# Softplus sums and a quantiser step shared between ScalarE, GpSimd and VectorE in a four-stage block kernel

## The chip, the cores and the metric
One core of a Trainium2 chip. The metric is the device time of one execution in microseconds (us): the median of the runs. The engines are TensorE (PE), VectorE (DVE), ScalarE (ACT), GpSimd (POOL) and SyncE (SP), which issues most DMAs.

## What is computed
The reference is a block of four layers on x (4 x 256 tokens of 256), each added with a gate tanh(g):

```python
x = x + tanh(g_xattn[0]) * L0_xattn(layernorm(x), ctx)   # softmax attention, keys and queries from ctx
x = x + tanh(g_ffn[0])   * L0_ffn(layernorm(x))          # silu(gate) * up, rms norm, projection
x = x + tanh(g_xattn[1]) * L1_xattn(ctx, layernorm(x))   # state space layer, 256 channels x 16 states
x = x + tanh(g_ffn[1])   * L1_ffn(layernorm(x))          # 64 experts, top 8
# two parts of it that the change touches:
delta = softplus(einsum('er,brl->bel', dt_proj_w, dt_lo) + dt_proj_b)      # of L1_xattn
scale = clip(mean(abs(w_g)), 1e-8); w_hat = clip(round(w_g / scale), -1, 1) * scale   # of L0_ffn, groups of 64
```

Softplus is computed as relu(v) + ln(1 + e) with e = exp(-|v|), plus a correction for what rounding 1 + e loses: c = (1 + e) - 1 - e, and delta = ln(1 + e) + (relu(v) - c). The ternary weights are computed in bf16: scale - |w|, a comparison of that with |w|, the sum of the two (the scale as rounded), then sign times mask, then times the scale.

## The kernel before
It is written by hand in one program per engine. Every wait and every order is explicit, and each engine runs its list in order, so an instruction that waits holds all behind it. A semaphore wait (`wait_ge`) names the count that must have been reached.

The time falls into a preparation (to about 70 us), the scan of the state space layer with the gated feed-forward layer beside it (to 200 us), the routing (to 230 us), and the 64 experts (to the end). The change lies in the preparation. Data is held with 128 rows on the partitions; the channels of the state space layer are two halves h of 128, with 1024 tokens each in the free dimension.

VectorE's list there: for half 0 the convolution (`convolve`, L1449 and three L1452, in place on `u`), the group sums and scales of the first weight part (`scales(0)`, L1458, L1460), eight maxima of the attention energies (L1489, out of PSUM), `convolve(1)`, `scales(1)`, the reciprocal of the softmax sums (L1493), then the quantiser: `rest_and_mask` (L1466 the difference scale - |w|, L1468 the comparison) for both parts, `restored` (L1474) for both, `quantised(0)` (L1481, L1483); then x1 (L1516, eight), statistics (L1417, L1420), the softplus steps `softplus_rest` (L1504 1 + e, L1506 the correction, L1509 relu minus it) for half 0, the same again for the second half of the tokens and half 1, then delta (L1526) for both halves, `quantised(1)`, four rests of the normalised tokens (L1534) and the first delta times u (L1539). From there `state(k)` runs 64 times: the product of delta u and B (L1556, in PSUM) and the scan (L1561), which needs ScalarE's decay (L853).

ScalarE's list: absolute weights (L743, L750), exponentials of the attention (L758), silu of u (L763, its second half after `convolve(1)`), normalising copies (L768, after L1493), signs of the weights (`signs`, L774), transposed attention (L779), Abs and Relu of the dt projection (L791, L792), Exp of both halves (L795), `signs(1)`, `normalised_rows(0)` (L785, waits for `nmr`, L1426), Ln (L800), `normalised_rows(1)`, `keep_high` (L818), two weight copies (L811), then `decay(0)` and on; `keep_middle` (L824) and a silu (L891) lie between the decays. An activation table is loaded (ACT_TABLE_LOAD) wherever the loaded set lacks the next function.

GpSimd's list: constants, `ln_rstd(1)` and `ln_rstd(2)` (L568, and L570, a power of -0.5) in two halves of the tokens each, two memsets, `rest_low` (L589), then the products of states and C (L602, `product`), with squares, hidden units and delta times u between.

TensorE's list: the attention energies (L1038), the x projection (L1045, which needs silu of u of both halves), attention transposes (L1052, which need L768), the dt projection (L1058), attention times values (L1065), weight transposes (L1077, L1089), token transposes (L1025), then the feed-forward layer (`gate_up`, L1153), which needs `rest_low`.

The second GpSimd operand of the difference is the scale, read with a stride of zero over pairs:

```python
in_pairs = "p (g n two) -> p g n two"
q_pairs, v_pairs = (v.rearrange(in_pairs, n=GROUP // 2, two=2) for v in (q_abs, q_v))
def over_group(part2):
    g = q_groups[part2]
    return part(q_scale[:, g.start, 0:1], (2, g.stop - g.start), (0, GROUP // 2), (1, 2))
```

## Time and profile before

| what | value |
|---|---|
| median of 3 runs | 410.79 us (410.63 to 410.82) |
| profiled execution | 411.59 us |
| its span, first to last instruction | 409.8 us |
| granted TensorE clock, mean | 0.928 |

The profiled execution is one of its own, and its parts are read against its own 411.59 us. A timeline row is a run of equal instructions: start, time from the first start to the last end, engine, line, operation, output and inputs, shapes, count, and in brackets how long the engine was idle before and who ended that. An instruction that is stopped after it has been issued shows that in its own duration. An instruction's end overlaps the next one's start a little, so sums are made from start to start.

### The profile page before, as it was taken

To read this page: it belongs to the slowest core of one execution; us is meant where nothing else is said; L and a number is where in the kernel's file an instruction comes from. 1 tells how busy PE (TensorE), PEld (TensorE's weight loads), DVE (VectorE), ACT (ScalarE), POOL (GpSimd) and SP (SyncE) were. 2 spreads that over 40 slices of the span, in tenths; PEclk is the share of its full clock that TensorE was granted. 3 is DMA by queue.
4 is the path that set the end of the run, shared out by engine and by line. 5 is a ranking of instruction groups with operands and counts; after the bars stand their busy time and mean duration, and the time that the engine had idled before them with its cause. 6 is when DMAs were issued, how large, how long until landed. Compare 5 with 4: busy or idle time off the path is not lost.

```text
span 409.8 us, 7559 instructions
## 1 busy us (share of the span) xinstructions
PE 335.7 (82%) x2206; PEld 269.0 (66%) x2217; DVE 305.5 (75%) x694; ACT 258.2 (63%) x528; POOL 260.6 (64%) x213
## 2 busy tenths in 40 slices
PE   4948944697798799799893299999999998999980
PEld 2433733365566567567793287998999897998960
DVE  2999999899999999999998937445453544454365
ACT  0998989999888888987265354445444443544410
POOL 4200041789978878887514678778878778787830
PEclk9997875799999989999899589999999999999995
DMA  8930520666435777331396349899888998865466
GB/s 233 375 123 14 155 102 0 219 229 220 155 114 186 258 264 251 129 136 51 85 268 175 112 103 247 204 230 225 214 217 213 233 224 194 215 146 91 84 123 226
DMA packets 59132, 72.17 MB, mean 176 GB/s; under 512 B 6802, under 2 KB 43458, under 8 KB 59106
## 3 DMA queue, kind: packets, MB, share of 16 engines
q1 hardware_dynamic: 49104, 56.04, 43.8%
q0 software_dynamic: 8832, 15.74, 19.2%
q8 instruction: 12, 0.20, 0.2%
q10 hardware_dynamic: 1170, 0.08, 0.2%
q14 instruction: 14, 0.11, 0.1%
HBM read 61.75 MB, written 10.09 MB: 175 GB/s over the span
## 4 chain that ended last, share of the span: by engine, by line
PE 43%; ACT 20%; DVE 15%; DMA 10%; issue 7%; POOL 2%; SPq 0%; DVEq 0%; POOLq 0%; ACTq 0%
PE bank L1319 12%; PE bank L1357 9%; PE bank L1312 5%; ACT ssm L853 4%; PE bank L1299 3%; DVE bank L1556 3%; ACT L853 3%; DMA ssm<-routed,idx 3%; ACT L891 3%; DVE ssm L1561 2%; DMA ssm<-bc_rows 2%; PE bank L1153 2%; DMA du<-sums 2%; DMA B_last<-bc_rows 2%; PE bank L1065 2%
## 5 line engine op out<-in xcount | busy, mean ns | idle before, releaser
L602 POOL TENSOR_TENSOR ssm<-ssm,arena 128x1024 f32<-128x1024 f32 x31 | 73.1, 2358 | 18.5 <-issue 10.2
L1561 DVE TENSOR_TENSOR_SCAN ssm<-ssm,bank 128x512 f32<-128x512 f32 x64 | 78.1, 1221 | 4.0 <-issue 1.8
L675 POOL DMA_INDIRECT ssm<-routed,idx x64 | 65.2, 1019 | 21.8 <-issue 14.6
L1784 DVE SCALAR_TENSOR_TENSOR ssm<-ssm,bank 128x96 f32<-128x96 f32 x64 | 20.0, 313 | 75.9 <-ACT ssm L965 75.7
L686 POOL DMA_INDIRECT sums<-ssm,idx x40 | 65.6, 1639 | 13.9 <-issue 10.4
L1319 PE MATMUL bank<-ssm,wguT 128*128 128x256 bf16 x576 | 72.4, 272 | 0.3 <-DVE ssm L1776 0.3
L1319 PEld LDWEIGHTS bank<-ssm,wguT 128*128 128x128 bf16 x576 | 56.0, 97 | 12.3 <-DVE ssm L1776 0.6
L965 ACT ACTIVATE ssm<-bank 128x96 f32<-128x96 f32 x64 | 16.0, 250 | 74.1 <-PE bank L1357 74.1
L1357 PE MATMUL bank<-arena,ssm 128*128 (+1 forms) x256 | 53.3, 331 | 1.6 <-ACT ssm L948 1.1
L1153 PE MATMUL bank<-xs,wguT 128*128 128x512 bf16 x182 | 44.4, 393 | 11.1 <-POOL xs L589 4.6
L853 ACT ACTIVATE ssm<-delta,A_sb 128x510 f32<-128x510 f32 x64 | 43.9, 713 | 6.8 <-DVE ssm L1561 6.7
L1095 PE MATMUL bank<-ident,ssm 128*128 128x128 f32 x256 | 35.1, 284 | 11.1 <-ACT bc_buf L860 5.8
L1357 PEld LDWEIGHTS bank<-arena,ssm 128*128 128x128 f32 x256 | 40.8, 193 | 3.4 <-issue 2.2
L568 POOL TENSOR_SCALAR rstd<-mv 128x4 f32<-128x4 f32 x8 | 2.7, 332 | 59.6 <-DVE mv L1420 48.4
L1153 PEld LDWEIGHTS bank<-xs,wguT 128*128 128x128 bf16 x192 | 18.8, 101 | 32.7 <-issue 8.9
L1095 PEld LDWEIGHTS bank<-ident,ssm 128*128 128x128 f32 x256 | 30.2, 146 | 15.1 <-ACT bc_buf L860 6.5
L1312 PE MATMUL bank<-arena,ssm 96*128 (+1 forms) x128 | 38.6, 383 | 0.5 <-ACT ssm L952 0.5
L1299 PE MATMUL bank<-ident,ssm 128*128 128x128 f32 x128 | 25.9, 285 | 5.9 <-DMA ssm<-routed,idx 5.9
L948 ACT ACTIVATE ssm<-bank 128x256 f32<-128x256 f32 x64 | 24.5, 383 | 9.2 <-PE bank L1299 9.1
L1556 DVE TENSOR_TENSOR bank<-bank,ssm 128x512 f32<-128x512 f32 x44 | 29.9, 679 | 0.1
L958 ACT ACTIVATE ssm<-bank 128x256 f32<-128x256 f32 x64 | 24.5, 383 | 6.4 <-PE bank L1312 3.5
L1299 PEld LDWEIGHTS bank<-ident,ssm 128*128 128x128 f32 x128 | 22.9, 198 | 6.8 <-DMA ssm<-routed,idx 6.6
(225 smaller groups left out, 663.7 us busy)
## 6 DMA issues: line engine op xcount, KB each, us to landing
ssm<-bc_rows SPq DMA_DIRECT2D x22, 512.0 KB, 3.7
arena<-bc_rows SPq DMA_DIRECT2D x16, 512.0 KB, 4.9
arena<-in_L_ffn_gate_proj SPq DMA_DIRECT2D x32, 192.0 KB
arena<-in_L_ffn_up_proj SPq DMA_DIRECT2D x32, 192.0 KB
arena<-in_L_ffn_down_proj SPq DMA_DIRECT2D x32, 192.0 KB
B_last<-bc_rows SPq DMA_DIRECT2D x10, 512.0 KB, 3.6
sums<-zero_f SPq DMA_DIRECT2D x1, 2304.0 KB, 14.1
arena<-in_L_ffn_w_gate_up SPq DMA_DIRECT2D x1, 2048.0 KB, 11.4
```

The lines of the kernel that those rows point to most:

```text
L602: pool.tensor_tensor(prod[:, a:b, :], hs[:, a:b, :], C_all[:, 2 * (q % 8):2 * (q % 8) + 2, :], ALU.mult).then_inc(s.prod_ok, 1)
L675: pool.indirect_dma_start(out=xe[:, k, :], out_offset=None, in_=routed, in_offset=bass.IndirectOffsetOnAxis(ap=idx2[:, k, 0:1], axis=0)).t ...
L686: pool.indirect_dma_start(out=sums, out_offset=bass.IndirectOffsetOnAxis(ap=idx2[:, k, 1:2], axis=0), in_=ye[:, k, :], in_offset=None, com ...
L853: act.activation(part(dA[:, k % 3, 0:1], (L, 2), (1, L - 1), offset=1), part(delta[:, h, 0:1], (L, 2), (1, L - 1), offset=th * 512 + 1), A ...
L1095: ins = pe.matmul(bank[3][:, t * P:t * P + P], prod[:, a, t * P:t * P + P], ident[:, :], start=first and t == 0, stop=False, is_transpose= ...
L1153: ins = pe.matmul(bank[(7, 0)[g]][:, :], wguT[:, kc, hc * P + g * H:hc * P + g * H + P], xs[:, part3, kc, th * 512:th * 512 + 512], start= ...
L1299: ins = pe.transpose(of_input()[:, t * P:t * P + P], part(xe[:, k, 0:1], (2, P), offset=t), ident[:, :])
L1312: pe.matmul(of_result(), hhT[0:I, k % 2, :], w_dn[:, bass.ds(slot, 1), :], start=True, stop=True).then_inc(s.m_y_ps, 1)
L1319: ins = pe.matmul(bank[4 + j // 2][:, (j % 2) * D:(j % 2) * D + D], places[:, which, j, :], ye_parts[:, which, c, :], start=False, stop=Fa ...
L1357: ins = pe.matmul(bank[1][:, 0:2 * I], xeT[:, k % 2, t * P:t * P + P], w_gu[:, :, bass.ds(slot, 1), t * I:(t + 1) * I], start=t == 0, stop ...
L1556: dve.tensor_tensor(x[:, :], bank[5][:, :], B_buf[q % 3][:, k % 2, :], ALU.mult).then_inc(s.dBu_ok, 1)
L1561: dve.tensor_tensor_scan(hs[:, k % 4, :], dA[:, k % 3, :], x[:, :], 0.0, ALU.mult, ALU.add).then_inc(s.scan_ok, 1)
```

## The change
- ScalarE loads the set of the exponential table ahead of its first wait, and the set `natural_log_exp_and_others` ahead of the Exp of softplus.
- 1 + e of both halves is made by ScalarE (Identity with a bias of 1) behind both Exp; VectorE's L1504 goes. VectorE keeps both corrections; half 0's subtraction and sum stay on VectorE, half 1's go to GpSimd, behind `ln_rstd(2)`. `decay` waits for half 0 at first and for half 1 at step 16.
- The quantiser's difference of the first weight part (4096 bf16 on 128 partitions) is made by GpSimd, behind `ln_rstd(1)`. The second part's stays on VectorE, behind the first comparison.
- The maxima and x1 are taken a PSUM bank at a time: four instructions of 512 for eight of 256.
- Semaphore counts follow (`q_step` without the differences, `q_rest`, `sp_one` and `delta_second` new; TensorE and ScalarE wait for the same data under the new counts).

Cut from the diff: the new semaphores' lines and the renumbered waits of ScalarE (`keep_high`) and TensorE.

```diff
--- before.py
+++ after.py
...
@@ -571,14 +574,26 @@
 
             ln_rstd(1)
 
+            g0 = q_groups[0]
+            pool.wait_ge(s.q_scales, 2)
+            pool.wait_ge(s.q_cast, 1)
+            pool.tensor_tensor(v_pairs[:, g0], over_group(0), q_pairs[:, g0], ALU.subtract).then_inc(s.q_rest, 1)
+
             ln_rstd(2)
+
+            pool.wait_ge(s.sp_c, 2)
+            pool.wait_ge(s.sp_relu, 4)
+            pool.tensor_tensor(Bbc[:, 1, :], du[:, 1, :], Bbc[:, 1, :], ALU.subtract).then_inc(s.delta_second, 1)
+            pool.wait_ge(s.delta_second, 1)
+            pool.wait_ge(s.sp_ln, 2)
+            pool.tensor_tensor(delta[:, 1, :], Cbc[:, 1, :], Bbc[:, 1, :], ALU.add).then_inc(s.delta_second, 1)
             pool.wait_ge(s.xm_ps, NT)
             for th in halves:
                 pool.memset(acc_sq[:, th, :], 0.0).then_inc(s.acc_ok, 1)
 
             def rest_of_du(h, t):
 
-                pool.wait_ge(s.delta_sb, 2)
+                pool.wait_ge(*((s.delta_sb, 1), (s.delta_second, 2))[h])
                 pool.wait_ge(s.u_sb, 2)
                 pool.tensor_tensor(du[:, h, t], delta[:, h, t], u[:, h, t], ALU.mult).then_inc(s.du_sb, 1)
 
...
@@ -715,6 +730,7 @@
             NCOLS = 16 * 4
 
 
+            act.preload_act_table_set("exp_and_others")
             act.wait_ge(s.c_pad, 1)
             for k in range(4):
                 act.wait_ge(s.xin_ps, k + 1)
...
@@ -754,7 +770,7 @@
                 act.activation(xnT[:, k % 2, (k // 2) * 512:(k // 2) * 512 + 512], bank[(5, 6, 7, 0)[k]][:, :], ACT.Copy).then_inc(s.xn1T_sb, 1)
 
             for j in range(NT):
-                act.wait_ge(s.en_max, 2 * (j // 2) + 2)
+                act.wait_ge(s.en_max, j // 2 + 1)
                 act.activation(att[:, j, :], bank[1 + j // 2][:, (j % 2) * L:(j % 2) * L + L], ACT.Exp, bias=nmax[:, j:j + 1],
                                accum_out=asum[:, j:j + 1]).then_inc(s.att_exp, 1)
 
...
@@ -790,9 +806,13 @@
                 src = bank[(7, 0, 5, 6)[k]][:, :]
                 act.activation(delta[:, h, c * 512:c * 512 + 512], src, ACT.Abs, bias=cols[:, 2 + h:3 + h]).then_inc(s.sp_abs, 1)
                 act.activation(du[:, h, c * 512:c * 512 + 512], src, ACT.Relu, bias=cols[:, 2 + h:3 + h]).then_inc(s.sp_relu, 1)
+            act.preload_act_table_set("natural_log_exp_and_others")
             for h in halves:
                 act.wait_ge(s.sp_abs, 2 * h + 2)
                 act.activation(delta[:, h, :], delta[:, h, :], ACT.Exp, scale=-1.0).then_inc(s.sp_exp, 1)
+            for h in halves:
+                act.wait_ge(s.sp_exp, h + 1)
+                act.activation(Bbc[:, h, :], delta[:, h, :], ACT.Identity, bias=1.0).then_inc(s.sp_one, 1)
             signs(1)
             normalised_rows(0)
             for h in halves:
...
@@ -842,12 +862,14 @@
             keep_quantised(1)
 
             act.wait_ge(s.Aneg, 2)
-            act.wait_ge(s.delta_sb, 2)
+            act.wait_ge(s.delta_sb, 1)
             act.wait_ge(s.reset_ok, 1)
 
             def decay(k):
 
                 th, h, n, t = of_step(k)
+                if k == DS:
+                    act.wait_ge(s.delta_second, 2)
                 if k >= 3:
                     act.wait_ge(s.scan_ok, k - 2)
                 act.activation(part(dA[:, k % 3, 0:1], (L, 2), (1, L - 1), offset=1),
...
@@ -1409,11 +1431,11 @@
 
                 for c in chunks:
                     if update:
-                        for j in range(4 * c, 4 * c + 4):
-                            update(j)
+                        for b in range(2 * c, 2 * c + 2):
+                            update(b)
                     for j in range(4 * c, 4 * c + 4):
-                        if update:
-                            dve.wait_ge(updated, j + 1)
+                        if updated:
+                            dve.wait_ge(updated, j // 2 + 1)
                         dve.bn_stats(stats[:, j, :], x_res[:, j, :]).then_inc(s.ln_stats, 1)
                     for j in range(4 * c, 4 * c + 4):
                         dve.wait_ge(s.ln_stats, 16 * (n - 1) + 4 * c + j + 1)
...
@@ -1462,31 +1484,32 @@
             def rest_and_mask(part2):
 
                 t, g = q_cols[part2], q_groups[part2]
-                dve.wait_ge(s.q_scales, 2 * part2 + 2)
-                dve.tensor_tensor(v_pairs[:, g], over_group(part2), q_pairs[:, g], ALU.subtract).then_inc(s.q_step, 1)
-                dve.wait_ge(s.q_step, 2 * part2 + 1)
+                if part2 == 1:
+                    dve.wait_ge(s.q_scales, 4)
+                    dve.tensor_tensor(v_pairs[:, g], over_group(1), q_pairs[:, g], ALU.subtract).then_inc(s.q_rest, 1)
+                dve.wait_ge(s.q_rest, part2 + 1)
                 dve.tensor_tensor(q_m[:, t], q_v[:, t], q_abs[:, t], ALU.is_lt).then_inc(s.q_step, 1)
 
             def restored(part2):
 
                 t = q_cols[part2]
-                dve.wait_ge(s.q_step, 2 * part2 + 2)
+                dve.wait_ge(s.q_step, part2 + 1)
                 dve.tensor_tensor(q_v[:, t], q_v[:, t], q_abs[:, t], ALU.add).then_inc(s.q_step, 1)
 
             def quantised(part2):
 
                 t = q_cols[part2]
                 dve.wait_ge(s.q_cast, part2 + 3)
-                dve.wait_ge(s.q_step, 6)
+                dve.wait_ge(s.q_step, 4)
                 dve.tensor_tensor(q_sign[:, t], q_sign[:, t], q_m[:, t], ALU.mult).then_inc(s.q_step, 1)
-                dve.wait_ge(s.q_step, 2 * part2 + 7)
+                dve.wait_ge(s.q_step, 2 * part2 + 5)
                 dve.tensor_tensor(q_r[:, t], q_v[:, t], q_sign[:, t], ALU.mult).then_inc(s.q_step, 1)
 
             convolve(0)
             scales(0)
-            for j in range(NT):
-                dve.wait_ge(s.en_ps, 2 * (j // 2) + 2)
-                dve.tensor_reduce(nmax[:, j:j + 1], bank[1 + j // 2][:, (j % 2) * L:(j % 2) * L + L], AX.X, ALU.max, negate=True).then_inc(s.en_max, 1)
+            for b in range(B):
+                dve.wait_ge(s.en_ps, 2 * b + 2)
+                dve.tensor_reduce(nmax[:, 2 * b:2 * b + 2], bank[1 + b][:, :].rearrange("p (a m) -> p a m", m=L), AX.X, ALU.max, negate=True).then_inc(s.en_max, 1)
             convolve(1)
             scales(1)
             dve.wait_ge(s.att_exp, NT)
...
@@ -1498,34 +1521,34 @@
 
             quantised(0)
 
-            def softplus_rest(h, meanwhile):
-
-                dve.wait_ge(s.sp_exp, h + 1)
-                dve.tensor_scalar(Bbc[:, h, :], delta[:, h, :], 1.0, None, ALU.add).then_inc(s.sp_c, 1)
-                dve.wait_ge(s.sp_c, 3 * h + 1)
+            def correction(h):
+
+                dve.wait_ge(s.sp_one, h + 1)
                 dve.scalar_tensor_tensor(out=Bbc[:, h, :], in0=Bbc[:, h, :], scalar=-1.0, in1=delta[:, h, :], op0=ALU.add, op1=ALU.subtract).then_inc(s.sp_c, 1)
-                dve.wait_ge(s.sp_c, 3 * h + 2)
-                dve.wait_ge(s.sp_relu, 2 * h + 2)
-                dve.tensor_tensor(Bbc[:, h, :], du[:, h, :], Bbc[:, h, :], ALU.subtract).then_inc(s.sp_c, 1)
-                meanwhile()
 
             dve.wait_ge(s.tg_sb, 1)
 
-            def x1(j):
-                dve.wait_ge(s.xm_ps, 2 * (j // 2) + 2)
-                dve.scalar_tensor_tensor(out=x_res[:, j, :], in0=bank[1 + j // 2][:, (j % 2) * L:(j % 2) * L + L], scalar=tg[:, 0:1],
-                                         in1=x_res[:, j, :], op0=ALU.mult, op1=ALU.add).then_inc(s.x1_sb, 1)
+            def x1(b):
+                dve.wait_ge(s.xm_ps, 2 * b + 2)
+                dve.scalar_tensor_tensor(out=x_res[:, 2 * b:2 * b + 2, :], in0=bank[1 + b][:, :].rearrange("p (a m) -> p a m", m=L), scalar=tg[:, 0:1],
+                                         in1=x_res[:, 2 * b:2 * b + 2, :], op0=ALU.mult, op1=ALU.add).then_inc(s.x1_sb, 1)
 
             statistics(2, x1, s.x1_sb, (0,))
-            softplus_rest(0, lambda: mean_over_deviation(2, 0))
-            statistics(2, x1, s.x1_sb, (1,))
-            softplus_rest(1, lambda: mean_over_deviation(2, 1))
-            for h in halves:
-                dve.wait_ge(s.sp_c, 3 * h + 3)
-                dve.wait_ge(s.sp_ln, h + 1)
-                dve.tensor_tensor(delta[:, h, :], Cbc[:, h, :], Bbc[:, h, :], ALU.add).then_inc(s.delta_sb, 1)
+            correction(0)
+            x1(2)
+            mean_over_deviation(2, 0)
+            x1(3)
+            statistics(2, None, s.x1_sb, (1,))
+            correction(1)
+            dve.wait_ge(s.sp_c, 1)
+            dve.wait_ge(s.sp_relu, 2)
+            dve.tensor_tensor(Bbc[:, 0, :], du[:, 0, :], Bbc[:, 0, :], ALU.subtract).then_inc(s.sp_c, 1)
+            mean_over_deviation(2, 1)
             quantised(1)
-            dve.wait_ge(s.q_step, 10)
+            dve.wait_ge(s.sp_c, 3)
+            dve.wait_ge(s.sp_ln, 1)
+            dve.tensor_tensor(delta[:, 0, :], Cbc[:, 0, :], Bbc[:, 0, :], ALU.add).then_inc(s.delta_sb, 1)
+            dve.wait_ge(s.q_step, 8)
             dve.memset(part(dA[:, 0, 0:1], (512, 3), (L, 2), (1, 1)), 0.0).then_inc(s.reset_ok, 1)
 
             for k in range(4):
...
```

## Rows read from the trace of the kernel before

**Rows 1.** The page: part 1 (busy us, share of the span), part 5 (costliest groups).
```profile
PE 335.7 (82%) x2206; PEld 269.0 (66%) x2217; DVE 305.5 (75%) x694; ACT 258.2 (63%) x528; POOL 260.6 (64%) x213
...
L602 POOL TENSOR_TENSOR ssm<-ssm,arena 128x1024 f32<-128x1024 f32 x31 | 73.1, 2358 | 18.5 <-issue 10.2
```

**Rows 2.** Timeline, VectorE, 24 to 35 us: start us, us, instruction.
```profile
24.68 2.73 DVE L1489 TENSOR_REDUCE nmax<-bank 128x1 f32<-128x256 f32 x8
27.33 0.80 DVE L1449 TENSOR_SCALAR u<-xin,conv_sb,cols 128x1024 f32<-128x1024 f32 x1
34.43 0.19 DVE L1493 RECIPROCAL rasum<-asum 128x8 f32<-128x8 f32 x1
34.54 2.24 DVE L1466 TENSOR_TENSOR ssm<-q_scale,arena 128x4096 bf16<-128x4096 bf16 x1
```

**Rows 3.** Timeline, VectorE, 54 to 82 us.
```profile
54.60 1.22 DVE L1509 TENSOR_TENSOR bc_buf<-du,bc_buf 128x1024 f32<-128x1024 f32 x1
70.11 0.70 DVE L1556 TENSOR_TENSOR bank<-bank,ssm 128x512 f32<-128x512 f32 x1
81.85 1.22 DVE L1561 TENSOR_TENSOR_SCAN ssm<-ssm,bank 128x512 f32<-128x512 f32 x1 [1.81 <-issue]
```

**Rows 4.** Timeline, ScalarE, 13 to 59 us; in brackets the idle time before.
```profile
13.29 0.60 ACT L721 ACTIVATE xin<-bank 128x512 f32<-128x512 f32 x1 [0.38 <-PE bank L1004]
32.12 1.06 ACT L763 ACTIVATE u<-u 128x1024 f32<-128x1024 f32 x1 [0.46 <-DVE u L1452]
34.66 1.71 ACT L768 ACTIVATE wguT<-wguT,rasum 128x256 f32<-128x256 f32 x4 [1.48 <-DVE rasum L1493]
50.25 2.00 ACT L795 ACTIVATE delta<-delta 128x1024 f32<-128x1024 f32 x2
55.93 2.08 ACT L785 ACTIVATE xw<-x_res,nmr,rstd 128x256 f32<-128x256 f32 x4 [1.88 <-DVE nmr L1426]
58.02 1.28 ACT L800 ACT_TABLE_LOAD   x1
```

**Rows 5.** The chain of waits, 68 to 80 us: start us, us, what.
```profile
68.20 1.28 ACT L853
79.75 1.28 ACT L853
```

**Rows 6.** Timeline, GpSimd: the price of its steps.
```profile
52.81 0.57 POOL L568 TENSOR_SCALAR rstd<-mv 128x4 f32<-128x4 f32 x1 [38.92 <-DVE mv L1420]
74.06 2.37 POOL L602 TENSOR_TENSOR ssm<-ssm,arena 128x1024 f32<-128x1024 f32 x1 [0.37 <-DVE ssm L1561]
86.76 1.15 POOL L589 TENSOR_TENSOR xs<-xnT,xs 128x512 bf16<-128x512 f32 x1
219.65 0.67 POOL L651 TENSOR_TENSOR xw<-delta,mask_b 128x256 f32<-128x256 f32 x1 [2.92 <-ACT delta L931]
```

**Rows 7.** Timeline, GpSimd and VectorE where they overlap, 53 to 231 us.
```profile
53.47 1.99 POOL L570 TENSOR_TENSOR rstd<-rstd,mhalf 128x4 f32<-128x4 f32 x1
...
196.83 2.35 POOL L602 TENSOR_TENSOR ssm<-ssm,arena 128x1024 f32<-128x1024 f32 x1
198.67 1.59 DVE L1617 TENSOR_TENSOR ssm<-ssm,arena 128x1024 f32<-128x1024 f32 x1
...
221.71 0.61 POOL L658 TENSOR_TENSOR xw<-xw,rasum 128x256 f32<-128x256 f32 x1
221.76 0.57 DVE L1426 SCALAR_TENSOR_TENSOR nmr<-mv,rstd 128x4 f32<-128x4 f32 x1 [0.39 <-POOL rstd L570]
...
226.32 1.71 DVE L1705 TENSOR_SCALAR bc_buf<-du 128x384 f16<-128x384 int16 x2
226.83 1.08 POOL L668 IOTA xin<- 128x1024 f16 x1
230.46 2.22 DVE L1705 TENSOR_SCALAR bc_buf<-du 128x384 f16<-128x384 int16 x11
```

**Rows 8.** Busy us by engine, 32 to 36 us; granted clock third from last.
```profile
32.00:36.00 4.00, 4.00 (x5) 0.78 (x5) 3.96 (x5) 2.40 (x5) 0.00 (x0) 0.50 0.00 0
```

More of the change, by code:

```diff
@@ L113, in __init__ @@
         self.q_scales = sem("q_scales")
+        self.q_rest = sem("q_rest")
         self.attT_ps = sem("attT_ps")
@@ L116, in __init__ @@
         self.sp_c = sem("sp_c")
+        self.sp_one = sem("sp_one")
+        self.delta_second = sem("delta_second")
         self.sp_ln = sem("sp_ln")
@@ L816, in keep_high @@
                 act.wait_ge(s.xn2T_ps, k + 1)
-                act.wait_ge(s.q_step, 8)
+                act.wait_ge(s.q_step, 6)
                 act.activation(xs[:, 0, kc, c], bank[1 + k][:, :], ACT.Copy).then_inc(s.xs_hi, 1)
@@ L1070, in _ @@
             pe.wait_ge(s.c_ident, 2)
-            pe.wait_ge(s.q_step, 8)
+            pe.wait_ge(s.q_step, 6)
             qv = q_r[:, q_cols[0]].rearrange("p (c d) -> p c d", d=D)
@@ L1078, in _ @@
                 ins.then_inc(s.quantT_ps, 1)
-            pe.wait_ge(s.x1_sb, NT)
+            pe.wait_ge(s.x1_sb, NT // 2)
             transpose_tokens(2, (1, 2, 3, 4), s.xn2T_ps)
-            pe.wait_ge(s.q_step, 10)
+            pe.wait_ge(s.q_step, 8)
             pv = q_r[:, q_cols[1]].rearrange("p (c h) -> p c h", h=H)
```

## The prediction
> **What bounds the kernel now.** The page's first part says little here: VectorE is busy 75% of the span [rows 1], and that is an average over stages. The change works between 24 and 80 us, so the views to read are the timelines of the engines over that stretch and the chain of waits. VectorE has no gap from 24.5 us to its scan at 81.85 us, the sixth [rows 2, 3]. ScalarE has only short waits, each for VectorE: 0.46 us for the second half's convolution, 1.48 us for the reciprocal of the softmax sums (L1493), 1.88 us for `nmr` [rows 4]. The chain agrees: ScalarE and TensorE carry it to about 49 us, then VectorE (x1, statistics, softplus), then ScalarE with a table load at 68.20 and one at 79.75 [rows 5]. The two engines run almost level, so a saving on VectorE alone buys little before 49 us and most of itself after. GpSimd is idle for 38.92 us, to 52.81 us [rows 6]. After 81.85 us nothing of the change is left and VectorE is dense again: what the sixth scan gains or loses is what the whole time gains or loses.
>
> **The change part by part.** All times are of the profiled execution, 411.59 us, of which 409.8 is its span; it lies 0.8 above the median of 410.79.
>
> **The first table preload**: the load before ScalarE's first copy moves ahead of a wait. The third copy waits 0.38 us for TensorE as it is [rows 4], so TensorE sets this start: 0. Without that cover at most 1.28 us would be gained.
>
> **The maxima**: eight reduces of 256 take 2.65 us from start to start (24.68 to 27.33 [rows 2]), 0.33 each. VectorE's two-input steps take 0.70 us for 512 elements and 1.22 for 1024 [rows 3], 1.02 ns for each more, so 256 more elements add 0.27: four take 4 x 0.60 = 2.40, -0.25. **x1 in pairs**: four fixed parts of about 0.13 fewer, -0.5, half of it before the first statistics. **Semaphore renumbering**, TensorE's waits on x1 and the `decay(16)` wait for the second half (29 us after the first state step): 0, the data is long there.
>
> **The quantiser's first difference on GpSimd** takes L1466's 2.24 us from VectorE [rows 2]. What does it cost GpSimd? A two-input f32 step takes 0.67 us for 256 elements (rows of 64) and 2.37 for 1024 [rows 6], 2.2 ns for each more; 4096 make 9.1 us. No row has an all-bf16 one: with one bf16 input and a bf16 output 512 take 1.15 [rows 6], 7% below that line (8.5 for ours); sixteen times the short one is 10.7. I take 8.9, nearer to the f32 line, and keep 8.5 to 10.7. It starts when the first scales are written, just after the first maximum starts at 24.68, so runs 24.85 to 33.75. The result is first needed at 34.2: on the face of it, it is hidden.
>
> **Whether it may run beside VectorE** is the step that decides. The collisions of [rows 7] show what happens when VectorE meets a GpSimd instruction that streams. L1617 (two SBUF inputs, 1024) started 198.67, GpSimd's product (196.83 + 2.35) ended 199.18, and it took 1.59 us where the same shape takes 1.22 (L1509 [rows 3]); it ended 1.08 after GpSimd. L1426, four elements, took 0.57, ending 0.01 after the GpSimd multiply of 221.71. A single-input f16 step (L1705) takes 0.2 in a row of 11 (2.22 us); the two beside a multiply's end and a 1.08 us iota took 1.71. Each time VectorE stood until GpSimd's instruction was over. What did not collide: VectorE's steps with one operand in PSUM. The 31 products average 2358 ns [rows 1] beside scans and state products, which all have one, and the one at 74.06 took 2.37 [rows 6]. In reverse GpSimd's `pow` of four elements, started at 53.47, ended at 55.46, 0.9 us after VectorE's L1506 had made way for L1509 at 54.60 [rows 3, 7].
> So I sort what stands behind 24.85 us on VectorE. The four maxima read PSUM: free, to 24.68 + 2.40 = 27.1. Then comes `convolve(1)`: L1449 does 1024 f32 elements in 0.80 us [rows 2], less than any two-input step (1.22), so like L1705 it runs in a faster single-input mode, and the three L1452 have two SBUF inputs. They stand until 33.75: 6.65 us, minus the 0.14 us of start-up that L1617 overlapped.
> The Trainium skill (SBUF — State Buffer, "SBUF: two separate sides") says the two engines' shared port pair is an exclusive lock held for the full instruction. The longest such hold in the trace is about 1 us; whether one of 9 us is held throughout no row shows, and the page's rule says yes. Without such a hold the sum would be that of rival A.
>
> **From there, by start-to-start times of before.** L1449 to the second scales took 27.33 to 34.43 [rows 2], 7.1 us; from 33.75, less 0.14, L1493 starts 40.7: +6.3. ScalarE's second silu and the normalising copies follow it: copies at 40.95 instead of 34.66. TensorE's second half of x_proj starts near 39.4 at the lower of the clock's levels, 1.2 GHz (0.50 in 32 to 36 us [rows 8], after TensorE had idled); three of its four matmuls then remain, and five half ones fill those 4 us, 0.85 each, so done 44.5; ScalarE wants it at 44.6. `signs(0)` starts 45.2, +6.4. From there ScalarE has no waits to the last Relu: 55.3.
> VectorE: masks, difference of part 1, restores to 49.0, `quantised(0)` to 53.5 (signs ready 48.8), two x1 to 54.9, statistics 56.4.
> ScalarE: load 56.6, two Exp 58.5, and now 1+exp: two more of 1024. Two Exp take 2.00 us [rows 4], so +0.95 each: 59.5 and 60.4; `signs(1)` 62.2. VectorE's `correction(0)` must wait for 59.5, a new stall of 3 us, which the late ScalarE makes and not the arithmetic; 60.8. Then x1(2), `nmr` 61.6, x1(3), statistics 63.85, `correction(1)` 65.1, the first half's subtraction 66.3. VectorE is rid of the two L1504 and of the second half's two sums, 2.4 us.
> ScalarE: rows of half 0 to 64.3, Ln to 66.25 without the load at 58.02, -1.28 [rows 4], diagonals 66.85.
> GpSimd: statistics ready 63.85; its `pow` is held by VectorE's two steps and ends 0.9 after the last of them, 67.2, as at 53.47. Next in its queue is the second half's subtraction, 2.36 us, whose inputs are ready; VectorE's `nmr` needs a semaphore first. That is the situation of L1426 at 221.76. So `nmr` 69.6 instead of 67.3. The last addition (2.36) then falls between the two steps of `quantised(1)`.
> ScalarE: rows of half 1 69.75 to 71.75, high parts 73.75, two weight copies 75.65, `decay(0)` 75.7 without the load at 68.20 (69.50 before: +6.2). VectorE: 69.65, L1481 70.9, GpSimd's addition 73.2, L1483 74.4, delta 75.6, four L1534 78.0, L1539 78.7, first state product 78.75 (70.11 before: +8.6). VectorE reaches the sixth scan 9.26 + 0.7 after that, 88.75; ScalarE reaches decay(5), behind decay(3), which waits for the first scan, at 87.7. Against 81.85 with 1.81 us of waiting: **+6.9 us**. C loads behind `signs(1)` (62.2 instead of 54) land 7 us before the first product; the other waits in GpSimd's queue (`rest_low` at 77.5) are behind nothing longer.
>
> The two saved loads are certain only if one set holds Exp and Ln. The loads at 58.02 and 68.20 show that they were taken from two sets. The Trainium skill (ScalarE: Activation LUTs, "Table sets: the hidden batching unit") says the named set has both; no row shows it. Without that the sum is +6.9 + 1.28 + 1.28 at most.
>
> Sum: 411.59 + 6.9 = 418.5 profiled, and by the same 0.8 a median of **417.7**.
>
> **The rivals.** **A, GpSimd and VectorE do not meet** (a long instruction lets go between pieces): the difference ends 33.75 before its use at 34.2. VectorE then gains 0.25 + 2.24 + 0.25 ahead of the first statistics, but `correction(0)` waits for ScalarE's 53.2, `signs(1)` ends 56.0 and the first rows start as before (55.93 [rows 4]). The gain is made after: Ln without load, rows of half 1 at 60.9 instead of 62.26, `decay(0)` 67.05 instead of 69.50, state 67.9 instead of 70.11. -2.4: 408.4. Against it: three collisions of [rows 7]; for it: none is longer than 1.1 us. Chance 9%.
> **B, only the long one holds.** `nmr` and `quantised(1)` slip past the two 1024 steps (`nmr` 67.3, state near 74.3): 6.9 - 2.7 = +4.2, 415.0. It would need VectorE to win each handover, where [rows 7] show it lose at 221.76. 14%.
> **C, the difference is far slower on GpSimd** than 10.7 us, its rows being pairs of bf16 beside a stride of zero. From 8.9 us on, each us is a us of stall. At twice the price, 17.8 us, 417.7 + 8.9 = 426.6. 10%.
> **D, the change does not do what it says** (preload ignored, one load back, ScalarE pieces longer): +1.3 to +2.6, 419 to 420.3. 5%.
>
> **How the numbers follow.** The forecast has 62%. Its bounds: the difference at 8.5 to 10.7 us (-0.4, +1.8), TensorE late at the low clock (x1 up to 0.7 later), B's mixture (-2.7) and D's loads (+2.6): 413.5 to 421. The range 413.0 to 421.5 leaves out A and C, about 2 in 10. 0.2% is 0.8 us, about what a measurement here can tell. Faster is A with something for other ways to gain, 0.10; same 0.03, a mixture between A and B; slower 0.87.
>
> **What would show it.** L1449 of the second half lasting some 7 us, or VectorE idle as long before it, ending with GpSimd's difference; that one's own length (8.5 to 10.7). L1493 at 40.7. `correction(0)` waiting for ScalarE. L1426 of the second half stretched by 2.3 us behind a GpSimd step. No table load between Exp and `decay(0)`. First state product near 78.8, sixth scan near 88.7. If L1449 keeps 0.80 us at 27.1, the prediction is wrong at its root, and A holds.

## The result and the profile after

The changed kernel takes 416.8 us (415.14 to 418.47, four runs) against 410.81 us (four runs of the kernel before beside them): a ratio of 1.0142 with an interval of 1.0101 to 1.0183, so +6.0 us, between +4.1 and +7.5. The forecast was 417.7 with a range of 413.0 to 421.5, and "slower" at 0.87. The profiled execution took 415.14 us (span 413.3); it is the quickest of the four, and this matters below.

The page, part 1 and the products of part 5, beside [rows 1]; and the busy table of 32 to 36 us beside [rows 8], in the same columns.

```profile
PE 338.0 (82%) x2206; PEld 266.7 (65%) x2217; DVE 307.4 (74%) x681; ACT 257.5 (62%) x528; POOL 272.8 (66%) x216
...
L617 POOL TENSOR_TENSOR ssm<-ssm,arena 128x1024 f32<-128x1024 f32 x31 | 73.1, 2359 | 19.4 <-DVE ssm L1584 11.4
...
32.00:36.00 4.00, 1.58 (x2) 0.00 (x0) 3.89 (x5) 0.00 (x0) 0.00 (x0) 0.50 0.00 0
```

VectorE ran 13 instructions fewer and was busy 1.9 us *longer*; GpSimd ran three more and was busy 12.2 us longer. The products beside the scans kept their length (2359 against 2358 ns), so the scan stage was left alone, as its operands in PSUM suggested. In 32 to 36 us ScalarE did nothing at all: it waited for the second half's convolution.

The place of the loss is VectorE's timeline, here beside [rows 2] (the maxima are now L1512, L1449 is L1471, L1493 is L1516), with GpSimd's difference.

```profile
24.25 2.47 DVE L1512 TENSOR_REDUCE nmax<-bank 128x2 f32<-128x512 f32 x4
26.64 5.37 DVE L1471 TENSOR_SCALAR u<-xin,conv_sb,cols 128x1024 f32<-128x1024 f32 x1
32.04 3.92 DVE L1474 SCALAR_TENSOR_TENSOR u<-xin,conv_sb,u 128x1024 f32<-128x1024 f32 x3
...
38.31 0.20 DVE L1516 RECIPROCAL rasum<-asum 128x8 f32<-128x8 f32 x1
...
24.41 7.05 POOL L580 TENSOR_TENSOR ssm<-q_scale,arena 128x4096 bf16<-128x4096 bf16 x1 [10.77 <-DVE q_scale L1482]
```

L1471, a step of 0.80 us before, lasts 5.37 and ends at 32.01, 0.55 us after GpSimd's difference (24.41 + 7.05 = 31.46). The timeline shows no idle time: a held instruction looks like a long one. The four maxima out of PSUM, under the same GpSimd instruction, were not held (2.47 us, the forecast's 2.40).

ScalarE, beside [rows 4]; GpSimd from 62 us, beside [rows 6, 7]; then VectorE from 57 us to the sixth scan, beside [rows 3].

```profile
5.86 1.28 ACT L733 ACT_TABLE_LOAD   x1 [5.86 <-issue]
...
12.76 0.60 ACT L737 ACTIVATE xin<-bank 128x512 f32<-128x512 f32 x1 [0.26 <-PE bank L1026]
...
36.00 1.06 ACT L779 ACTIVATE u<-u 128x1024 f32<-128x1024 f32 x1 [4.48 <-DVE u L1474]
...
53.13 1.28 ACT L809 ACT_TABLE_LOAD   x1
...
56.33 1.99 ACT L815 ACTIVATE bc_buf<-delta 128x1024 f32<-128x1024 f32 x2
...
61.99 1.99 ACT L820 ACTIVATE bc_buf<-delta 128x1024 f32<-128x1024 f32 x2
...
72.92 1.34 ACT L875 ACTIVATE ssm<-delta,A_sb 128x510 f32<-128x510 f32 x2
```

```profile
62.89 1.86 POOL L573 TENSOR_TENSOR rstd<-rstd,mhalf 128x4 f32<-128x4 f32 x1
64.73 2.33 POOL L586 TENSOR_TENSOR bc_buf<-du,bc_buf 128x1024 f32<-128x1024 f32 x1
67.15 3.29 POOL L589 TENSOR_TENSOR delta<-bc_buf 128x1024 f32<-128x1024 f32 x1
...
74.86 2.71 POOL L604 TENSOR_TENSOR xs<-xnT,xs 128x512 bf16<-128x512 f32 x2 [3.50 <-ACT xs L844]
```

```profile
57.41 1.23 DVE L1527 SCALAR_TENSOR_TENSOR bc_buf<-bc_buf,delta 128x1024 f32<-128x1024 f32 x1 [3.25 <-ACT bc_buf L815]
...
64.79 2.29 DVE L1448 SCALAR_TENSOR_TENSOR nmr<-mv,rstd 128x4 f32<-128x4 f32 x1 [0.94 <-POOL rstd L573]
67.01 1.21 DVE L1504 TENSOR_TENSOR xs<-xs,ssm 128x2048 bf16<-128x2048 bf16 x1
68.26 3.26 DVE L1506 TENSOR_TENSOR arena<-ssm,xs 128x2048 bf16<-128x2048 bf16 x1
...
74.98 1.58 DVE L1562 TENSOR_TENSOR bank<-delta,u 128x512 f32<-128x512 f32 x1
76.66 0.70 DVE L1579 TENSOR_TENSOR bank<-bank,ssm 128x512 f32<-128x512 f32 x1
...
86.62 1.22 DVE L1584 TENSOR_TENSOR_SCAN ssm<-ssm,bank 128x512 f32<-128x512 f32 x1
```

Three more steps of VectorE are stretched beside a GpSimd instruction: `nmr` of four elements 2.29 us, L1506 3.26 instead of 1.22, delta times u (L1562) 1.58 instead of 0.69. The load in front of the first decay (68.20 in [rows 5]) is gone from ScalarE's timeline; the one of 79.75, behind the silu between the decays, is still there, at 84.21. The chain of waits can be followed back only to 73.86 us in this trace; its second row is the stretched delta times u:

```profile
73.86 1.20 DVE xnT L1557 x2
75.06 1.51 DVE bank L1562
```

The first state product starts 6.55 us later than before (76.66 against 70.11) and the sixth scan 4.77 later (86.62 against 81.85 [rows 3]); before, 1.81 us of the way between them had been waiting.

### The profile page after: what moved, and what is told of

Its sections match the earlier page's. It is cut to its first block, busy times and chain, and to the rows that moved or that the text cites. A ratio compares the mean times of both kernels' runs of the same rounds, so it can differ in the third digit from the quotient of the medians.

```text
span 413.3 us, 7551 instructions
## 1 busy us (share of the span) xinstructions
PE 338.0 (82%) x2206; PEld 266.7 (65%) x2217; DVE 307.4 (74%) x681; ACT 257.5 (62%) x528; POOL 272.8 (66%) x216
## 4 chain that ended last, share of the span: by engine, by line
PE 36%; DVE 12%; ACT 12%; issue 8%; DMA 7%; POOL 5%; SPq 0%; DVEq 0%; POOLq 0%; ACTq 0%
PE bank L1341 10%; PE bank L1379 8%; PE bank L1334 5%; ACT ssm L875 3%; PE bank L1175 3%; DVE bank L1579 3%; PE bank L1321 3%; DVE ssm L1584 3%; DMA ssm<-routed,idx 3%; ACT L875 2%; ACT L913 2%; POOL ssm L690 2%; PE bank L1117 2%; PE bank L1327 1%; DMA du<-sums 1%
## 5 line engine op out<-in xcount | busy, mean ns | idle before, releaser
L617 POOL TENSOR_TENSOR ssm<-ssm,arena 128x1024 f32<-128x1024 f32 x31 | 73.1, 2359 | 19.4 <-DVE ssm L1584 11.4
L701 POOL DMA_INDIRECT sums<-ssm,idx x40 | 65.9, 1648 | 13.9 <-issue 10.7
L1175 PE MATMUL bank<-xs,wguT 128*128 128x512 bf16 x182 | 47.3, 412 | 7.1 <-POOL xs L604 2.8
L1117 PE MATMUL bank<-ident,ssm 128*128 128x128 f32 x256 | 33.8, 278 | 11.0 <-ACT bc_buf L882 5.7
L1117 PEld LDWEIGHTS bank<-ident,ssm 128*128 128x128 f32 x256 | 29.4, 143 | 15.4 <-POOL ssm L617 6.9
L1321 PE MATMUL bank<-ident,ssm 128*128 128x128 f32 x128 | 25.9, 284 | 5.6 <-DMA ssm<-routed,idx 5.5
L1321 PEld LDWEIGHTS bank<-ident,ssm 128*128 128x128 f32 x128 | 22.8, 198 | 6.7 <-DMA ssm<-routed,idx 6.5
```

The costliest lines, as they stand in the source:

```text
L617: pool.tensor_tensor(prod[:, a:b, :], hs[:, a:b, :], C_all[:, 2 * (q % 8):2 * (q % 8) + 2, :], ALU.mult).then_inc(s.prod_ok, 1)
L701: pool.indirect_dma_start(out=sums, out_offset=bass.IndirectOffsetOnAxis(ap=idx2[:, k, 1:2], axis=0), in_=ye[:, k, :], in_offset=None, com ...
L1117: ins = pe.matmul(bank[3][:, t * P:t * P + P], prod[:, a, t * P:t * P + P], ident[:, :], start=first and t == 0, stop=False, is_transpose= ...
L1175: ins = pe.matmul(bank[(7, 0)[g]][:, :], wguT[:, kc, hc * P + g * H:hc * P + g * H + P], xs[:, part3, kc, th * 512:th * 512 + 512], start= ...
L1321: ins = pe.transpose(of_input()[:, t * P:t * P + P], part(xe[:, k, 0:1], (2, P), offset=t), ident[:, :])
```

## The experiments

All of them keep or add work; none leaves any out. The measure in the traces is the start of the sixth scan, which has VectorE dense behind it; the end of the span is blurred by the expert stage, whose length differs by 1 to 2 us between the traces (188.0 us from the last `nmr` to the end before, 186.8 after, 186.0 in diff_back). Two theories went in: that of the forecast, in which GpSimd holds VectorE (H), and one in which ScalarE, made longer by 1 + e, causes the loss (L).

**diff_back**: only the first difference returns to VectorE.

```diff
-            pool.tensor_tensor(v_pairs[:, g0], over_group(0), q_pairs[:, g0], ALU.subtract).then_inc(s.q_rest, 1)
...
-                if part2 == 1:
...
+                dve.tensor_tensor(v_pairs[:, g], over_group(part2), q_pairs[:, g], ALU.subtract).then_inc(s.q_rest, 1)
```

> The changed kernel with the first difference back on VectorE (in front of the first comparison), all else as changed. Theory H (a streaming GpSimd instruction holds VectorE's two-port steps to its end): L1449 of the second half is back at 0.80 us, the reciprocal of the softmax sums starts near 34.1 instead of 38.3, the nmr step behind GpSimd's subtraction still takes some 2.3 us, first state product near 72.4, sixth scan +0.5 against before, time about 411.3. Rival L (the loss is made by 1+exp on ScalarE, which lets the first correction wait 3.25 us): the wait stays 3 us and the time stays near 415 to 417.

Measured: 411.53 us (ten runs), ratio 1.0031 (1.0008 to 1.0054). Sixth scan +0.41. GpSimd, then VectorE, 58 to 72 us:

```profile
58.55 1.86 POOL L573 TENSOR_TENSOR rstd<-rstd,mhalf 128x4 f32<-128x4 f32 x1
60.38 2.33 POOL L581 TENSOR_TENSOR bc_buf<-du,bc_buf 128x1024 f32<-128x1024 f32 x1
...
60.44 2.30 DVE L1443 SCALAR_TENSOR_TENSOR nmr<-mv,rstd 128x4 f32<-128x4 f32 x1 [0.93 <-POOL rstd L573]
```

1 + e is still on ScalarE here, and 4.4 of the 4.77 us are gone, which speaks against L. The meeting at `nmr` stays although everything is 4.4 us earlier: it is made by the order of GpSimd's list, not by the late start.

**sums_back**: the opposite, half 1's subtraction and sum return to VectorE and the difference stays on GpSimd.

```diff
-            pool.tensor_tensor(Bbc[:, 1, :], du[:, 1, :], Bbc[:, 1, :], ALU.subtract).then_inc(s.delta_second, 1)
...
-            pool.tensor_tensor(delta[:, 1, :], Cbc[:, 1, :], Bbc[:, 1, :], ALU.add).then_inc(s.delta_second, 1)
...
+            dve.tensor_tensor(Bbc[:, 1, :], du[:, 1, :], Bbc[:, 1, :], ALU.subtract).then_inc(s.delta_second, 1)
...
+            dve.tensor_tensor(delta[:, 1, :], Cbc[:, 1, :], Bbc[:, 1, :], ALU.add).then_inc(s.delta_second, 1)
```

> The changed kernel with the second half's two softplus sums back on VectorE, behind those of the first half; GpSimd keeps the difference. H: nmr of the second tokens takes 0.15 us and comes 2.3 us sooner, the second step of quantised(1) is back at 1.22 us, first state product near 74.0 instead of 76.7 although VectorE has 2.4 us more to do, time about 414.2. If the two holds near 65 to 71 us cost nothing on the path: 416.8 plus up to 2.4 us, since VectorE gets the work back.

Measured: 414.0 us (five runs), ratio 1.0089 (1.0048 to 1.013). Sixth scan +3.49.

```profile
65.42 0.16 DVE L1442 SCALAR_TENSOR_TENSOR nmr<-mv,rstd 128x4 f32<-128x4 f32 x1 [0.94 <-POOL rstd L573]
65.50 1.22 DVE L1498 TENSOR_TENSOR xs<-xs,ssm 128x2048 bf16<-128x2048 bf16 x1
66.76 1.22 DVE L1500 TENSOR_TENSOR arena<-ssm,xs 128x2048 bf16<-128x2048 bf16 x1
```

Without the two GpSimd steps `nmr` takes 0.16 us and L1500 (after's L1506) 1.22: both stretches were theirs.

**diff_alone**: nothing but the difference on GpSimd, in the kernel before; 1 + e stays on VectorE and the table loads stay.

```diff
+            pool.tensor_tensor(v_pairs[:, g0], over_group(0), q_pairs[:, g0], ALU.subtract).then_inc(s.q_rest, 1)
...
+                if part2 == 1:
+                    dve.wait_ge(s.q_scales, 4)
...
+                else:
+                    dve.wait_ge(s.q_rest, 1)
```

> The kernel before with one part of the change: the first difference on GpSimd. H: L1449 of the second half lasts about 5.4 us and ends with GpSimd's difference, reciprocal +3.9, and after 2.24 us given back and 1 us of waiting for the Exp the state steps start 2.9 us late: about 413.7. Rival L: no 1+exp on ScalarE here, so 408.6 to 410.8.

Measured: 414.27 us (four runs), ratio 1.0094 (1.0069 to 1.012). Sixth scan +3.28. VectorE and GpSimd:

```profile
27.28 5.11 DVE L1455 TENSOR_SCALAR u<-xin,conv_sb,cols 128x1024 f32<-128x1024 f32 x1
...
24.79 7.05 POOL L578 TENSOR_TENSOR ssm<-q_scale,arena 128x4096 bf16<-128x4096 bf16 x1 [10.83 <-DVE q_scale L1466]
```

This ends L as the cause of the loss: the difference alone, with ScalarE's list untouched, costs 3.6 us, and L1455 again ends 0.55 us after it (32.39 and 31.84).

**both_back**: the changed kernel without either GpSimd part (the two edits above together), so table preloads, 1 + e on ScalarE and the bank-wide steps alone.

```diff
-            pool.tensor_tensor(v_pairs[:, g0], over_group(0), q_pairs[:, g0], ALU.subtract).then_inc(s.q_rest, 1)
...
-            pool.tensor_tensor(Bbc[:, 1, :], du[:, 1, :], Bbc[:, 1, :], ALU.subtract).then_inc(s.delta_second, 1)
```

> The changed kernel with neither GpSimd part: the difference and the second half's sums are VectorE's again; 1+exp on ScalarE, the tables and the steps by whole banks stay. H: no VectorE step is held by more than some tenths of a us; the wait of the first correction for 1+exp stays (0.8 us); first state product near 70.4, sixth scan near 80.3 instead of 81.85, time about 409.1. If ScalarE's extra work is what costs: no less than 410.7.

Measured: 409.84 us (12 runs), ratio 0.9972 (0.995 to 0.9994). Sixth scan -1.41; GpSimd's `rest_low` (L593) and VectorE's delta times u (L1556):

```profile
68.68 2.72 POOL L593 TENSOR_TENSOR xs<-xnT,xs 128x512 bf16<-128x512 f32 x2 [7.25 <-ACT xs L833]
...
68.93 1.46 DVE L1556 TENSOR_TENSOR bank<-delta,u 128x512 f32<-128x512 f32 x1
```

The first state product (70.48) and the sixth scan (80.44) came within 0.2 us of what was expected; the median is 0.7 us above it, which this stretch does not explain. Yet a collision that no theory named is there: ScalarE, rid of its loads, gives `rest_low` its input before VectorE has passed delta times u, which then stands 0.77 us. From there to the sixth scan VectorE has no gap.

**tables_only**: the kernel before with the two preloads.

```diff
+            act.preload_act_table_set("exp_and_others")
...
+            act.preload_act_table_set("natural_log_exp_and_others")
```

> The kernel before with the two table loads placed by hand and nothing else. The loads in front of Ln and of the first decay go. VectorE is the later engine up to the first state product, so that stays at 70.1; the sixth scan, which waits 1.8 us for ScalarE, comes 1.3 to 1.8 us sooner: about 409.3. If the set in question cannot serve both, or the sign and identity steps, the loads stay and the time is 410.7.

Measured: 409.23 us (12 runs), ratio 0.9966 (0.9941 to 0.9991). Sixth scan -1.38. ScalarE and VectorE:

```profile
57.96 1.99 ACT L802 ACTIVATE bc_buf<-delta 128x1024 f32<-128x1024 f32 x2
...
68.11 1.34 ACT L855 ACTIVATE ssm<-delta,A_sb 128x510 f32<-128x510 f32 x2
...
80.47 1.22 DVE L1563 TENSOR_TENSOR_SCAN ssm<-ssm,bank 128x512 f32<-128x512 f32 x1 [0.39 <-DVE bank L1558]
```

Two lines give all of the gain of both_back within their intervals. Both loads (2.56 us) are gone, the first state product did not move (70.16 against 70.11, VectorE being dense before it), and the gain came out of the wait before the sixth scan, 1.81 us before and 0.39 now: 1.42 of 2.56.

**diff_split**: the changed kernel with the difference in four GpSimd instructions of 1024 elements.

```diff
+            for piece in range(4):
+                gp = slice(16 * piece, 16 * piece + 16)
...
+                pool.tensor_tensor(v_pairs[:, gp], scale_p, q_pairs[:, gp], ALU.subtract).then_inc(s.q_rest, 1)
```

> The changed kernel with the difference in four GpSimd instructions of 1024 elements. H, hold by instruction with a handover at each end: L1449 is held only to the end of the piece that runs (under 2.5 us in all instead of 5.4), and then one or more of the three L1452 are stretched by a piece of 1.8 us each; the convolution ends near 36 as before the split, the time stays within 1 us of the changed kernel's. If GpSimd keeps the ports while it has work: L1449 lasts 5.4 us again and the three others are at 1.28 us each.

Measured: 417.07 us, one run. VectorE, then GpSimd:

```profile
27.25 2.08 DVE L1473 TENSOR_SCALAR u<-xin,conv_sb,cols 128x1024 f32<-128x1024 f32 x1
29.36 6.96 DVE L1476 SCALAR_TENSOR_TENSOR u<-xin,conv_sb,u 128x1024 f32<-128x1024 f32 x3
36.24 2.28 DVE L1482 TENSOR_REDUCE q_sum<-arena 128x32 f32<-128x2048 bf16 x1
...
25.02 8.91 POOL L582 TENSOR_TENSOR ssm<-q_scale,arena 128x1024 bf16<-128x1024 bf16 x4 [11.00 <-DVE q_scale L1484]
```

Neither engine goes on alone: VectorE gets in between two pieces, one step at a time, so what is held is let go at the end of an instruction. The convolution takes 9.0 us (27.25 to 36.24) where the changed kernel's takes 9.2 (26.64 to 35.88): the stalls are only spread over three steps. And the difference itself takes 8.91 us instead of 7.05 because GpSimd now waits as well. Splitting gains nothing in this one run (sixth scan +5.11 against +4.77).

**write_beside, write_first, read_one**: what kind of GpSimd instruction holds what kind of VectorE step. Each adds one to the kernel before, into memory that is written over later: a memset of 4096 f32 behind L1449 (so beside the three L1452), the same memset 0.2 us ahead of L1449, and an addition of a constant to 4096 bf16 ahead of L1449. VectorE also waits for the added instruction in front of the reciprocal, where it has been over for 2.7 us or more in all three.

```diff
+            pool.wait_ge(s.conv, 5)
+            pool.memset(ssm_flat[:, 0:4096], 0.0).then_inc(s.q_rest, 1)
```

In write_first the same memset waits for `en_max` at 7 instead, and read_one has behind that wait:

```diff
+            pool.tensor_single_scalar(q_v[:, 0:4096], q_abs[:, 0:4096], 1.0, op=ALU.add).then_inc(s.q_rest, 1)
```

> The kernel before with one GpSimd memset of 4096 f32 (a scratch that is written later anyway) that starts when L1449 of the second half is done, so beside the three two-input steps L1452 and the group sums. It reads nothing. If any GpSimd instruction that streams holds VectorE's two-input steps, the first L1452 lasts 4 us longer; if only one that reads does, the three keep 1.28 us each and the memset its 4 us. The Trainium skill (SBUF - State Buffer, two separate sides) says of two-input steps that only a GpSimd instruction that reads SBUF holds them.

> Adds to the kernel before a GpSimd memset of 4096 f32 elements that starts when the seventh maximum is written, near 27.1 us, so that VectorE's L1449 (one SBUF input, start 27.33, 0.80 us) falls inside it; in write_beside the same memset took 3.51 us and ran beside the two-input L1452, which kept their length. Question: did the iota hold the single-input f16 step in the kernel before because VectorE's faster single-input mode is held by any streaming GpSimd instruction, or because of something else? Theory M (the single-input mode is held even by a GpSimd instruction that only writes): L1449 lasts until the memset's end, 27.1 + 3.5 = 30.6, so about 3.3 us, the reciprocal moves by 2.4. Theory N (only a GpSimd instruction that reads SBUF holds VectorE): L1449 keeps 0.80 us and the reciprocal stays at 34.3.

> Adds to the kernel before a GpSimd addition of a constant to 4096 bf16 elements (one SBUF input instead of two, bf16 output), started when the seventh maximum is written, near 27.1 us. Theory R (any GpSimd instruction that reads and writes SBUF in a stream holds VectorE's L1449 and L1452 until it is over): L1449 lasts to its end; with no row for a one-input bf16 step I take 1.7 ns an element as the two-input difference took, 7 us, as the high end and the memset's 0.86 ns, 3.5 us, as the low end, so the convolution ends 2.4 to 6 us later. Theory T (only a GpSimd instruction with two SBUF inputs holds VectorE): L1449 keeps 0.80 and the three L1452 3.93 us, and the reciprocal stays at 34.3.

Measured (one run each): 411.25, 412.75 and 421.21 us; sixth scan -0.13, +2.93 and +10.37. VectorE and GpSimd of the three in turn:

```profile
28.03 3.93 DVE L1456 SCALAR_TENSOR_TENSOR u<-xin,conv_sb,u 128x1024 f32<-128x1024 f32 x3
...
28.05 3.51 POOL L576 MEMSET ssm<- 128x4096 f32 x1 [14.12 <-DVE u L1453]
```

```profile
27.19 3.87 DVE L1453 TENSOR_SCALAR u<-xin,conv_sb,cols 128x1024 f32<-128x1024 f32 x1
31.09 3.92 DVE L1456 SCALAR_TENSOR_TENSOR u<-xin,conv_sb,u 128x1024 f32<-128x1024 f32 x3
...
27.00 3.51 POOL L576 MEMSET ssm<- 128x4096 f32 x1 [13.27 <-DVE nmax L1493]
```

```profile
27.47 11.04 DVE L1454 TENSOR_SCALAR u<-xin,conv_sb,cols 128x1024 f32<-128x1024 f32 x1
38.54 3.92 DVE L1457 SCALAR_TENSOR_TENSOR u<-xin,conv_sb,u 128x1024 f32<-128x1024 f32 x3
...
27.38 10.58 POOL L577 TENSOR_SCALAR ssm<-arena 128x4096 bf16<-128x4096 bf16 x1 [13.40 <-DVE nmax L1494]
```

Theory M holds for the memset (3.87 us, not 0.80), and R in its part on L1449 for the one-input addition, whose length, 10.58 us, lay beyond the high end of 7. The same 3.51 us memset left three two-input steps at 3.93, though two of the three started inside it. So there are two classes on VectorE. The single-input step in its faster mode (0.80 us for 1024) is held by a GpSimd instruction that only writes; a step with two SBUF inputs is held by one that reads (diff_split, 6.96 instead of 3.92) and not by one that only writes. Whether a one-input reader holds a two-input step no run shows: in read_one the L1457 start behind it. The Trainium skill (SBUF — State Buffer, "Who interferes with whom") states this pair of rules; these rows agree with both halves.

**placed**: diff_back with half 1's subtraction between the two halves of `ln_rstd(2)`, where VectorE has x1 (one input in PSUM) and statistics (one input) to do, and half 1's sum behind the scan's first product. To make room, VectorE's `nmr` and second correction now stand ahead of the two x1 of the second half of the tokens, so VectorE's order changes too.

```diff
-            ln_rstd(2)
-
+            ln_rstd(2, (0,))
...
+            ln_rstd(2, (1,))
...
+                if f == 0:
...
+                    pool.tensor_tensor(delta[:, 1, :], Cbc[:, 1, :], Bbc[:, 1, :], ALU.add).then_inc(s.delta_second, 1)
...
+            mean_over_deviation(2, 0)
+            correction(1)
             x1(2)
-            mean_over_deviation(2, 0)
             x1(3)
             statistics(2, None, s.x1_sb, (1,))
-            correction(1)
```

> The difference on VectorE; the second half's subtraction on GpSimd while VectorE does x1 out of PSUM and statistics, its sum on GpSimd behind the first product of the scan, where VectorE's operands lie in PSUM; nmr is put ahead of the second correction. H: no VectorE step is held by the two, both GpSimd steps keep 2.3 us, first state product near 68.2, sixth scan near 79.9, time about 408.7, below both kernels. If GpSimd beside VectorE costs whatever VectorE does, L1527 and the statistics or the first products and scans are stretched, and nothing is gained over the kernel without GpSimd's parts.

Measured: 408.47 us (12 runs), ratio 0.9945 (0.9926 to 0.9963); it is faster than both kernels. VectorE, then GpSimd, 57 to 78 us:

```profile
57.00 1.41 DVE L1529 SCALAR_TENSOR_TENSOR x_res<-bank,tg,x_res 128x512 f32<-128x512 f32 x2
58.32 1.40 DVE L1436 BATCH_NORM_STATS2 stats<-x_res 128x6 f32<-128x256 f32 x4
...
68.37 0.69 DVE L1558 TENSOR_TENSOR bank<-delta,u 128x512 f32<-128x512 f32 x1
...
57.16 2.36 POOL L580 TENSOR_TENSOR bc_buf<-du,bc_buf 128x1024 f32<-128x1024 f32 x1 [1.84 <-DVE bc_buf L1523]
...
75.41 2.35 POOL L636 TENSOR_TENSOR delta<-bc_buf 128x1024 f32<-128x1024 f32 x1
```

The same two GpSimd steps that cost 1.82 us in the changed kernel's order (sixth scan of diff_back against both_back) hold nothing here: x1 and statistics beside the first and the state products and scans beside the second have their free lengths, and both steps take the unhindered 2.36 and 2.35. `rest_low` starts at 70.28 here, behind delta times u (68.37), so that collision is gone as well. The first state product starts at 69.15 and the sixth scan at 80.94, each 1 us later than expected; this execution reached the second half's convolution 1.41 us late (28.74 against 27.33 [rows 2]). In front of the sixth scan VectorE waits 1.85 us for ScalarE's decay: VectorE's gain has made ScalarE the later engine there. Against tables_only (409.23) the gain of 0.8 us is not separated from none, nor is the 1.4 us against both_back (409.84): the intervals of the ratios overlap.

## Why the prediction was right, and what was mis-sized

The sixth scan in the traces, and the medians:

| kernel | sixth scan starts | against before | median against before |
|---|---|---|---|
| before | 81.85 | | |
| both_back | 80.44 | -1.41 | ratio 0.9972 |
| both_back + sums (diff_back) | 82.26 | +0.41 | 1.0031 |
| both_back + difference (sums_back) | 85.34 | +3.49 | 1.0089 |
| both_back + both (the change) | 86.62 | +4.77 | 1.0142 |

The rest gains 1.41; the sums cost 1.82 and the difference 4.90, each net of what it saves on VectorE; together they cost 6.18, 0.54 less than their sum.

**The decisive step held.** GpSimd and VectorE meet, and the held step stands to the end of the GpSimd instruction for as long as that lasts: L1471 takes 5.37 us here, the same step 11.04 in read_one, both instead of 0.80; the holds in the trace of before were of about 1 us. Rival A (no meeting) falls with L1471. Rival B (only the long one holds) falls with `nmr` at 2.29 and L1506 at 3.26. Rival D falls with the loads: one at 53.13, none before L820 and `decay(0)` (the Trainium skill, ScalarE: Activation LUTs, "Table sets: the hidden batching unit", has exp and ln in the one set, and the trace agrees), and L815 takes two times 1.0 us as its price said. Rival C fell on the other side: the difference was not slower than 10.7 us but faster than 8.5.

**The mis-sized term** is GpSimd's price for the difference: "4096 make 9.1 us ... I take 8.9 ... and keep 8.5 to 10.7". It took 7.05, 1.72 ns an element, below the lower end. The nearest row (one bf16 input, 1.15 us for 512) was 7% below the f32 line, and I took that 7% as the most that a step with bf16 on both sides would save; it saved 22%. This is 1.85 us, and it runs through the whole forecast: with 0.44 from an earlier start the reciprocal came at 38.31 instead of 40.7. ScalarE waited 4.48 us before the second silu and, as before, 1.48 for the reciprocal. TensorE's second half of the x projection was told to end just as ScalarE wants it; ScalarE waited 0.18 us for it (42.50). `signs(0)` started at 42.99 instead of 45.2, the wait of the first correction was 3.25 us (told: 3), 1 + e ready at 57.4 instead of 59.5, `pow` over 0.9 after VectorE's second step, `nmr` held 2.29 (told: 2.3), the addition came between the two steps of `quantised(1)`. First state product 76.66 instead of 78.75, sixth scan 86.62 instead of 88.75: each 2.1 early.

**One stall was missed**, and hides in that 2.1: delta times u, 0.89 us behind `rest_low` (1.58 instead of 0.69). At its start VectorE was 3.0 us earlier than forecast (74.98 against 78.0): 2.3 of this from the difference and its start, 0.7 from small steps since. I had `rest_low` at 77.5 as "behind nothing longer" and did not ask which VectorE step it would run beside; it came at 74.86. VectorE has no gap from there to the sixth scan, so up to 0.89 us of the +4.77 are this stall, and up to 0.77 in both_back; ScalarE may have been next in line, so the bound is not a measurement.

**The two saved loads** are worth 1.4 us when nothing else changes, not 2.56: in tables_only the first state product is unmoved, since VectorE was dense before it, and only the 1.81 us of waiting could be won. This does not test rival A's 408.4, which had VectorE relieved of work as well. placed, with the difference on VectorE, comes near A's sum: the first state product at 69.15 in an execution that was 1.41 us late, against 67.9, and a median of 408.47. What was wrong in A is that it let the two engines overlap freely.

**The end.** The sum for this execution was 418.5; it took 415.14: 2.1 of the 3.4 us are those above, and 1.3 lie in the experts: the changed kernel is 4.70 us behind before at the last `nmr` of the routing (226.46 against 221.76 [rows 7]) and 3.5 at the end of the span (413.3 against 409.8). The other three runs were 0.7 to 3.3 us longer than the traced one, so the median, 416.8, is closer to the forecast than the mechanism was: 0.9 us off at the median, 2.1 at the sixth scan. That closeness at the median is luck. The 0.8 us that I took off for profile against median had the wrong sign here (median 1.7 above the profiled run). Where the other runs spent their time no trace shows; +4.77 us lies within the interval of +4.1 to +7.5. The inner bounds of 413.5 to 421 do not come out of the terms listed for them either: added up, these give 414.6 to 422.8.

## What to carry to other kernels

Before moving a step from VectorE to an idle GpSimd, list what VectorE does in the same stretch by the kind of its operands: single-input steps in the fast mode, and steps with two SBUF inputs if the GpSimd instruction reads SBUF, stand until that instruction is over, while steps with an input in PSUM, reduces of PSUM and statistics kept their lengths in every trace here. An output in PSUM is not enough: delta times u writes there, reads both inputs from SBUF, and was stretched. Beside the second kind a shared step was free, as in placed, though what it gains then depends on the next engine in line; beside the first VectorE stands for what is left of it, however idle GpSimd looks, and cutting it in pieces did not help. In a timeline look for an instruction that is longer than its shape and ends just after one of the other engine: such a stall was shown as busy time in these traces, and not as waiting.

## What the runs showed of the hardware that I had not expected

- GpSimd's all-bf16 two-input step takes 1.72 ns an element (7.05 us for 4096) where the f32 one takes 2.30 (2.36 us for 1024); the one-input bf16 addition of a constant takes 2.58 (10.58 us for 4096), more than the two-input one. No run shows why.
- A GpSimd memset (0.86 ns an element, 3.51 us for 4096 f32) holds VectorE's fast single-input step, 3.87 us instead of 0.80, though it reads nothing, and leaves two-input steps alone.
- A held step ends 0.55 us after the GpSimd instruction where it would take 0.80 alone (write_first, read_one, diff_alone, the change). So about 0.25 us of its work seems to be done before the wait, which is inferred and not measured.
- Four elements suffice to be held: `nmr` 2.29 us instead of 0.16. So a small step of VectorE behind a long one of GpSimd costs what is left of the long one.
